# Several experts' numbers in one whole number, taken apart in registers, in both expert stages

## The reference, cut to what matters

```
# 8 experts, the best 2 of each row
t1  = einsum('td,efd->tef', flat, mlp1_w) + mlp1_b
y   = einsum('tei,edi->ted', swiglu(t1), mlp2_w) + mlp2_b
out = sum(take_along_axis(y, idx) * wts)              # idx, wts: the row's top 2

# 64 experts, the best 8 of each row
h   = silu(xf @ W1[e] + B1[e]) @ W2[e] + B2[e]        # for each expert e
acc = acc + sum(where(ti == e, tw, 0)) * h            # tw, ti: the row's top 8
out = acc + the two shared experts
```

## Time and profile before

| what | |
|---|---|
| median of three runs | 1419.27 us (1418.36 to 1423.72) |
| the profiled execution, its own time | 1419.37 us |
| its span, first to last instruction | 1417.2 us |
| mean granted TensorE clock | 0.975 |
| busy: PE, DVE, ACT | 1287.6, 981.6, 879.6 us |
| chain that ended last | PE 67%, DVE 13%, DMA 6%, ACT 5%, issue 5%, ACTq 2% |

### The profile page before, as it was taken

How to read it: one execution, slowest core, us unless ns; L and a number is a source line. 1 busy time by engine, 2 the same in 40 slices (tenths; PEclk the granted TensorE clock), 3 DMA queues, 4 the chain that set the end, 5 groups by cost and what they waited for, 6 DMA issues and landing times.

```text
span 1417.2 us, 28347 instructions
## 1 busy us (share of the span) xinstructions
PE 1287.6 (91%) x9262; PEld 997.0 (70%) x9262; DVE 981.6 (69%) x2767; ACT 879.6 (62%) x2147; POOL 436.8 (31%) x457
## 2 busy tenths in 40 slices
PE   7999998998999979999999999999888888878993
PEld 6899897885556556666766766676677776767893
DVE  7767774575556758987787887988547544766665
ACT  5556663334766657777877775777246666666540
POOL 0000001243154251410010000775118733444574
PEclk9999999999999989999999999999979999999997
DMA  9522201423465120324432400231638877888343
GB/s 346 201 73 82 76 13 39 141 81 117 141 206 187 61 83 14 123 76 155 147 128 98 144 18 5 98 121 61 269 98 269 281 245 221 251 251 245 100 131 100
DMA packets 147626, 194.64 MB, mean 137 GB/s; under 512 B 14639, under 2 KB 129941, under 8 KB 146453
## 3 DMA queue, kind: packets, MB, share of 16 engines
q1 hardware_dynamic: 132117, 150.79, 32.4%
q0 software_dynamic: 15360, 41.96, 9.4%
HBM read 107.77 MB, written 84.93 MB: 136 GB/s over the span
## 4 chain that ended last, share of the span: by engine, by line
PE 67%; DVE 13%; DMA 6%; ACT 5%; issue 5%; ACTq 2%; POOL 1%; SPq 0%; DVEq 0%; POOLq 0%
PE PS L72 9%; PE PS L74 8%; PE PS L73 8%; PE PS L3279 6%; PE PS L1416 5%; PE PS L3251 5%; DMA xt_z<-zs 4%; PE PS L2458 4%; PE PS L2479 3%; PE PS L3266 3%; PE PS L3294 3%; PE PS L1432 2%; DVE a_pt L971 2%; PE PS L2448 2%; PE PS L1310 2%
## 5 line engine op out<-in xcount | busy, mean ns | idle before, releaser
L3401 ACT ACTIVATE c_pt<-PS 100x512 f32<-100x512 f32 x256 | 138.8, 595 | 90.8 <-PE PS L3266 90.2
L3392 ACT ACTIVATE c_pr<-c_sm,c_mn 128x400 f32<-128x400 f32 x256 | 158.8, 627 | 18.6 <-DVE c_mn L3541 18.6
L2458 PE MATMUL PS<-xt_zt,xt_w1c 128*128 128x128 f32 x760 | 124.4, 288 | 37.8 <-ACT xt_w1c L2556 36.2
L3541 DVE CUSTOM_DVE_ANT_0 c_sm<-PS,c_mw 128x400 f32<-128x400 f32 x256 | 135.8, 567 | 11.4 <-PE PS L3251 9.8
L2458 PEld LDWEIGHTS PS<-xt_zt,xt_w1c 128*128 128x128 f32 x760 | 102.9, 197 | 49.9 <-ACT xt_w1c L2556 47.4
L3279 PE MATMUL PS<-c_pt,c_v 100*64 100x512 f32 x512 | 125.7, 612 | 0.0
L3251 PEld LDWEIGHTS PS<-c_k,c_q 64*128 64x128 f32 x768 | 62.3, 187 | 83.0 <-issue 49.6
L2479 PE MATMUL PS<-xt_w,xt_h 128*128 x380 | 115.6, 387 | 0.3 <-DVE xt_y L2645 0.3
L3251 PE MATMUL PS<-c_k,c_q 64*128 64x400 f32 x768 | 105.5, 380 | 9.3 <-DVE c_mn L3541 8.7
L449 POOL TENSOR_TENSOR rs<-ve,halfneg 128x4 f32<-128x4 f32 x12 | 13.8, 1146 | 324.7 <-DVE ve L464 231.1
L3550 DVE TENSOR_SCALAR c_pr<-c_pr,c_rl 128x400 f32<-128x400 f32 x256 | 106.9, 459 | 4.5
(11 more groups left out here) (404 smaller groups left out, 3516.5 us busy)
## 6 DMA issues: line engine op xcount, KB each, us to landing
ys<-xt_y SPq DMA_DIRECT2D x190, 128.0 KB
xt_z<-zs SPq DMA_DIRECT2D x46, 512.0 KB, 4.8
zs<-x_zero SPq DMA_DIRECT2D x14, 1536.0 KB, 6.7
xt_w<-x_w SPq DMA_DIRECT2D x4, 2048.0 KB, 15.3
a_cT<-ctxT SPq DMA_DIRECT2D x4, 1601.0 KB
a_raw_nat<-ctx SPq DMA_DIRECT2D x4, 1536.0 KB
zs<-e_zero SPq DMA_DIRECT2D x2, 2944.0 KB, 22.0
ys<-e_y SPq DMA_DIRECT2D x46, 128.0 KB
```

The source lines that it names most:

```text
L2458: last = pe.matmul(PS[:, 2 + q % 2, 0:P], xt_w1c[q % 3][:, k, :], xt_zt[q % 4][:, k, :], start=k == 0, stop=k == KD - 1)
L3392: act.activation(c_pr[s % 3][h][:, :], c_sm[h][:, :], ACT.Exp, bias=c_mn[:, s % 4, h:h + 1], scale=-1.0, accum_out=c_l[:, s % 4, h:h + 1]) ...
L3401: act.activation(c_pt[u % 2][0:KW, :, :, i * P + r * DH:i * P + (r + 1) * DH].rearrange("p h t q -> p (h t) q"), PS[0:KW, BT + r, :].rearr ...
L3541: dve.tensor_tensor_reduce(c_sm[h][:, :], PS[:, BS + h, 0:WIN], c_mw[:, b * QT + i, :], 1.0, BIG, ALU.add, ALU.min, c_mn[:, s % 4, h:h + 1 ...
```

## The change

A table entry now holds several numbers side by side, as digits of one whole number. Stage 1 packs eight blocks' experts (three bits each), so a half of 23 blocks has three entries; PE and ACT load all three when the half begins, and take a block's expert out with a shift and a mask in registers (the first of an entry needs only the mask). Stage 2 packs four tiles' pairs (five bits each): at every fourth tile one value is loaded and tested, and each tile takes its pair out. The packing is done by DVE in floats, with steps that multiply the right neighbour by a power of two and add: `table` has five more operations per half, `x_tables_in` four. In the built program PE's register instructions of the kind REGISTER_ALU go from 91 to 509 and ACT's from 46 to 322, and TENSOR_LOAD from 95 to 55 on each.

```diff
+PACKS = -(-NB // 8)
-        e_of = sb("e_of", [1, GR, 24], I32)
+        e_of = sb("e_of", [1, GR, PACKS], I32)
+        e_pk = sb("e_pk", [1, PACKS, 8])
-        PL = 16
+        PL = 21
+        def packed_experts(eng, g):
+            return [eng.value_load(e_of[0:1, g, c:c + 1], min_val=0, max_val=E0 ** 8 - 1) for c in range(PACKS)]
+        def expert_of(packed, q):
+            g, n = q // NB, q % NB
+            return (packed[g][n // 8] >> (E0 - 1).bit_length() * (n % 8)) & (E0 - 1)
...
             def first(q):
-                expert[q] = pe.value_load(e_of[0:1, g, n:n + 1], min_val=0, max_val=E0 - 1)
+                if n == 0:
+                    packed[g] = packed_experts(pe, g)
+                expert[q] = expert_of(packed, q)
...
             def prefill(q):
-                expert[q] = act.value_load(e_of[0:1, g, n:n + 1], min_val=0, max_val=E0 - 1)
+                if n == 0:
+                    packed[g] = packed_experts(act, g)
+                expert[q] = expert_of(packed, q)
...
             def table(g):
-                dve.tensor_copy(e_of[:, g, 0:NB], PS[0:1, 7, 128:128 + NB]).then_inc(SP_["planned"], 1)
+                dve.memset(row[:, NB:], 0.0).then_inc(SP_["planned"], 1)
+                dve.tensor_copy(row[:, 0:NB], PS[0:1, 7, 128:128 + NB]).then_inc(SP_["planned"], 1)
+                for n, j in enumerate((1, 2, 4)):
+                    dve.scalar_tensor_tensor(at[:, :, 0], at[:, :, j], float(E0 ** j), at[:, :, 0], ALU.mult, ALU.add
+                                             ).then_inc(SP_["planned"], 1)
+                dve.tensor_copy(e_of[:, g, :], e_pk[:, :, 0]).then_inc(SP_["planned"], 1)
...
-        def four_pairs(engine, at):
-            return nc.values_load_multi_w_load_instructions(at, engines=[engine], min_val=0, max_val=NP - 1)[1]
+        def four_pairs(eng, at):
+            packed = eng.value_load(at, min_val=0, max_val=(1 << 4 * FIELD) - 1)
+            return [(packed >> FIELD * j) & (NP - 1) for j in range(4)]
...
-                    four = four_pairs(mybir.EngineType.Activation, x_of[g][0:1, n:n + 4])
+                    four = four_pairs(act, x_of[g][0:1, n // 4:n // 4 + 1])
```

More of the change, by code:

```diff
@@ L329, in build_program @@
         x_xb = x_kept(224, NX, lambda v: v)
-        x_of = x_kept(320, 4 * NXC, lambda v: v[0:1, :].bitcast(I32))
+        x_of = x_kept(320, NXC, lambda v: v[0:1, :].bitcast(I32))
         x_top = x_kept(416, 64, eights)
@@ L1401, in turned @@
                 last.then_inc(SP_["t"], 1)
-            expert = {}
+            expert, packed = {}, {}
             def first(q):
@@ L1792, in table @@
                 dve.wait_ge(SP_["counted"], 3 * g + 3)
-                dve.tensor_copy(e_of[:, g, 0:NB], PS[0:1, 7, 128:128 + NB]).then_inc(SP_["planned"], 1)
+                s = PLAN[g] + 15
+                row = e_pk[:, :, :].rearrange("p c n -> p (c n)")
+                dve.memset(row[:, NB:], 0.0).then_inc(SP_["planned"], 1)
+                dve.tensor_copy(row[:, 0:NB], PS[0:1, 7, 128:128 + NB]).then_inc(SP_["planned"], 1)
+                for n, j in enumerate((1, 2, 4)):
+                    dve.wait_ge(SP_["planned"], s + 2 + n)
+                    at = e_pk[:, :, :].rearrange("p c (m j) -> p (c m) j", j=2 * j)
+                    dve.scalar_tensor_tensor(at[:, :, 0], at[:, :, j], float(E0 ** j), at[:, :, 0], ALU.mult, ALU.add
+                                             ).then_inc(SP_["planned"], 1)
+                dve.wait_ge(SP_["planned"], s + 5)
+                dve.tensor_copy(e_of[:, g, :], e_pk[:, :, 0]).then_inc(SP_["planned"], 1)
             def routed(b):
@@ L1953, in build_program @@
         PIECES = 7
-        PL_N, OWN_N = 11, 7
+        PL_N, OWN_N = 11, 11
+        FIELD = (NP - 1).bit_length()
         BIG23 = float(1 << 23)
@@ L2210, in x_tables @@
             wait_from(pe, XR["out"], g * PIECES + 5)
-            wait_from(pe, XR["own_of"], (g + 1) * OWN_N)
+            wait_from(pe, XR["own_of"], g * OWN_N + 7)
             pe.matmul(PS[:, bank, 0:P], x_bs[:, :], ident[:, :], start=True, stop=True)
@@ L2218, in x_tables_in @@
             dve.tensor_copy(x_thr[g], PS[:, bank, 0:NX])
-            dve.tensor_copy(x_of[g], PS[0:1, bank, P:P + 4 * NXC])
+            dve.tensor_copy(x_bs[0:1, 0:4 * NXC], PS[0:1, bank, P:P + 4 * NXC]).then_inc(XR["own_of"][0], 1)
+            pairs = x_bs[0:1, 0:4 * NXC].rearrange("p (c n) -> p c n", n=4)
+            own = g * OWN_N + 7
+            wait_from(dve, XR["own_of"], own + 1)
+            for h in range(2):
+                dve.scalar_tensor_tensor(pairs[:, :, 2 * h], pairs[:, :, 2 * h + 1], float(1 << FIELD), pairs[:, :, 2 * h],
+                                         ALU.mult, ALU.add).then_inc(XR["own_of"][0], 1)
+            wait_from(dve, XR["own_of"], own + 3)
+            dve.scalar_tensor_tensor(pairs[:, :, 0], pairs[:, :, 2], float(1 << 2 * FIELD), pairs[:, :, 0],
+                                     ALU.mult, ALU.add).then_inc(XR["own_of"][0], 1)
+            wait_from(dve, XR["own_of"], own + 4)
+            dve.tensor_copy(x_of[g], pairs[:, :, 0])
             dve.tensor_copy(x_ohT[:, :], PS[0:NP, bank, 2 * P:3 * P]).then_inc(XR["out"][0], 1)
@@ L2468, in owner @@
                 if n % 4 == 0:
-                    four = four_pairs(mybir.EngineType.PE, x_of[g][0:1, n:n + 4])
+                    four = four_pairs(pe, x_of[g][0:1, n // 4:n // 4 + 1])
                     for j in range(4):
```

## The result

The changed kernel takes 1402.95 us (median of 4 runs, 1401.37 to 1407.45), the kernel before 1419.05 beside it. The ratio is 0.9885, with a 95% interval of 0.9853 to 0.9916: 16.1 us less (12 to 21 by that interval), where 14.4 less (1405) had been forecast. The profiled execution took 1401.96 us with a span of 1399.8.

The account below looks back on a forecast made before the run. ACT's sequencer was taken as the bound: its loads and range tests delay the weights' copy PE awaits in stage 2. Terms -28.5 + 9 + 3 + 2 = -14.5 took 1419.4 to 1405 us, range 1397 to 1412.

Parts of the forecast that it names:

- The tests that go: Stage 2, ACT: three of four range tests and a narrower load save 0.62 us per group, 28.5 us over 46.
- The steps that come: Stage 2, other three tiles: two register steps and the address need 0.26 us, all covered, so they cost nothing.
- The cover of 0.33: Stage 2, ACT: 0.28 us under the turned rows' copy plus 0.05 slack behind it hide sequencer work at each tile.
- Rows, +9: Stage 2: the rows' load window shrinks from 5.14 to 4.52 us, so PE waits longer for rows, +9 us.
- Longer landing and stores: Stage 2: transfers crowd into less time; landings grow 0.1 us (+2) and stores of results come closer (+1), together +3.
- Tables and stage 1: DVE's added table operations cost +1 us in the first half, stage 1's loads and steps +1 us.
- PE's waits for the weights' copy: Stage 2 sign: PE's waits for ACT's weights copy fall from 36.2 to between 6 and 18 us.
- The rival that the loads take the gain: Stage 2: landings grow by 0.5 us, giving 1414, or by 0.75, giving 1419; chance 0.15.

Follow-up runs that it names:

- rows and stores relieved: Changed kernel with each chunk's rows load issued two tiles earlier and six result buffers instead of four: 1386.1 us; the kernel before with the same edits: 1412.85 us.
- the kernel with six steps: Changed kernel with six register steps instead of two on ACT at each of the three tiles without a load: 1405.54 us.
- the kernel with all three edits: Changed kernel with ACT's load and test ahead of the turned rows' copy, rows loads issued two tiles earlier, six result buffers instead of four: 1375.48 us.
- the kernel with the load ahead and rows earlier: Changed kernel with ACT's load and test ahead of the turned rows' copy and rows loads issued two tiles earlier: 1389.71 us.

## Why the prediction was right

The change was forecast at -14.4 us and came to -16.1, by the steps named. Point by point:

- *The tests that go, -28.5.* From the rows' copy to the weights' 0.73 was forecast, and the trace's median is 0.70; 0.37 per group are still lost in the median where 0.40 were forecast. With rows and stores relieved the packing is worth 26.75, tables included, and the sum without its transfers has 28.5 - 2 = 26.5.
- *The steps that come, nothing.* Right: 38 ns each, 0.28 at the other tiles. The cover of 0.33 is borne out by the kernel with six steps; the price of steps beyond it was too high, since one tile of three pays and not each.
- *Rows, +9.* PE's waits for them rose by 7.0, to 13.9 where some 16 were forecast; issued two tiles earlier, the waits and 9.5 us are gone.
- *Longer landing and stores, +3.* The stores were mis-sized: 1 us was put down for them, while DVE's waits for them rose by 8.0 and PE's for results from 0.3 to 3.6. A landing grew by about the 0.1 us assumed: by the semaphore events of the two traces its median goes from 4.6 to 4.8 us in the first half and from 5.4 to 5.5 in the second. All that the transfers took back together is 8 to 11 us, where 9 + 3 were forecast. That the rows came out a little cheaper than forecast and the stores dearer is luck, of 2 or 3 us.
- *Tables and stage 1, +2.* Stage 2's first multiplication starts 0.9 later; stage 1 alone cannot be told from nothing.
- *PE's waits for the weights' copy* were to be 6 to 18 us and are 3.8, in 14 instead of 46 waits. PE's weight loads show the rest. A line of the page of the kernel before, and one of the waits after:

```profile
L2458 PEld LDWEIGHTS PS<-xt_zt,xt_w1c 128*128 128x128 f32 x760 | 102.9, 197 | 49.9 <-ACT xt_w1c L2556 47.4
```

```profile
PEld PS L2495 <- ACT xt_w1c L2593: 17.9, 47, 0.7
```

They waited 47.4 us for that copy and now wait 17.9, which is 29.5 less beside the 28.5 of the sum; 17.9 / 47 = 0.38 per load of pairs is what the sum went by (0.40). PE's own waits are shorter than those of its weight loads, before as after (36.2 against 47.4, 3.8 against 17.9).

The rival that the loads take the gain asked for landings longer by 0.5 us or more. They grew by 0.05 to 0.2, and 8 to 11 of some 26 us were taken back, not nearly all. The Trainium skill (DMA: Bandwidth & Descriptors, section "Latency and other measured facts") has a floor of about 600 ns for a `tensor_load`. No floor of that kind shows here: the packed value's load takes 272 to 278 ns at the least and in the median of the second half. Single loads of 600 ns and more occur (below).

## What to carry to other kernels

Register work that stands behind an engine's last wait begins only when that wait is over: in both traces ACT's load of pairs starts 6 ns after the rows' copy, in the median. What the instruction ahead does not cover of it is then serial with the engine. Price it by the pitch of its register instructions (0.07 us for a step and 0.23 for a range test here), and first ask whether it can stand ahead of the wait, which here was worth another 10 us or so (1386.1 to 1375.5) once transfers were in time. When a stage gets faster, every transfer that is issued a fixed number of tiles ahead loses that time from its window: move its issue or add a buffer with the change, and judge the change with that done, or part of its worth (8 to 11 of some 26 us here) does not show. A wait that disappears from one engine's list may only have been covered by the next one, so two edits are best tried in all four combinations.

## What the runs showed of the hardware that had not been expected

The same load of registers from on-chip memory takes 0.27 us or up to four times as much, depending on when it starts. In the changed kernel ACT's loads of the first half take 291 ns in the median and 597 at most. With rows issued two tiles earlier, and in the kernel with all three edits, they take:

```profile
L2407 ACTq TENSOR_LOAD <-R x24: 274/422/1075, 1031.3 to 1159.8; - x24
```

```profile
L2407 ACTq TENSOR_LOAD <-R x24: 272/536/1167, 1034.1 to 1157.7; - x24
```

The shortest stay at 272 to 274, so it is something that they meet and not the instruction that costs. The rows' transfer into that memory is one candidate: in the kernel before 29 of the 48 loads start within 0.6 us behind its issue, with rows issued earlier most start 1.2 to 3 us behind it. It does not explain all, since rows come in the second half as well. There the kernel with the load ahead and rows earlier has short loads, and the one with six buffers on top has long ones:

```profile
L2407 ACTq TENSOR_LOAD <-x_keep x24: 272/278/502, 1164.2 to 1281.2; - x24
```

```profile
L2407 ACTq TENSOR_LOAD <-x_keep x24: 276/428/655, 1161.1 to 1268.0; - x24
```

In both, most of these start 1.2 to 1.8 us behind an issue (16 and 20 of 24). So other transfers or POOL's work beside them may count too. The cause stays open; no run took a transfer away and left the load where it was.
